# Graph layers: the receivers' offsets made in two parts, first head first

## The reference, cut to what matters

```python
def gat_conv(x, src, dst, W, att_src, att_dst, bias):
    N = x.shape[0]
    h = (x @ W).reshape(N, HEADS, HID)            # HEADS 4, HID 256, N 1250
    a_src = jnp.sum(h * att_src, axis=-1)
    a_dst = jnp.sum(h * att_dst, axis=-1)
    e = jax.nn.leaky_relu(a_src[src] + a_dst[dst], NEG_SLOPE)      # 0.2
    m = jax.ops.segment_max(e, dst, num_segments=N)
    e = jnp.exp(e - m[dst])
    s = jax.ops.segment_sum(e, dst, num_segments=N)
    alpha = e / (s[dst] + 1e-16)
    msg = alpha[:, :, None] * h[src]
    out = jax.ops.segment_sum(msg, dst, num_segments=N)
    return out.reshape(N, HEADS * HID) + bias
```

## Time and profile before

| what | value |
|---|---|
| median of 3 runs | 2343.44 us (2342.75 to 2345.57) |
| the profiled execution | 2332.56 us |
| its span | 2330.8 us |
| TensorE matmuls busy | 1995.9 us, 86% of the span |
| VectorE busy | 1480.5 us, 64% |
| ScalarE busy | 1132.7 us, 49% |
| layer 1, from its first rows to its last step | about 1336 to 1636 us |
| layer 2 | about 1636 to 1989 us |

### The profile page before, as it was taken

The page is one execution under the profiler, slowest core; times in us unless marked ns, Lnnn a source line. Parts: engine busy times, 40 slices in busy tenths (PEclk is TensorE's granted clock), DMA queues, the critical chain, the costliest instruction groups (busy, mean ns, idle before and its releaser), DMA issues. The chain is left out here.

```text
span 2330.8 us, 36639 instructions
## 1 busy us (share of the span) xinstructions
PE 1995.9 (86%) x11260; PEld 1284.6 (55%) x11261; DVE 1480.5 (64%) x2465; ACT 1132.7 (49%) x2288; POOL 794.3 (34%) x630
## 2 busy tenths in 40 slices
PE   5899999999996829999975597999999999980997
PEld 2444444444444727777732444777344777540997
DVE  1299999999995874333348675777373777438011
ACT  5777777777773314555510514665002666210332
POOL 4188888888880012444453000000000000001453
PEclk9999999999998957999988698999999999995998
DMA  5565565555552424778544313000012100331894
GB/s 162 168 164 154 153 155 156 155 155 154 155 155 80 93 82 147 264 254 261 186 127 125 103 44 116 22 22 1 18 44 89 57 22 1 109 110 35 227 275 93
DMA packets 200742, 285.13 MB, mean 122 GB/s; under 512 B 116698, under 2 KB 128677, under 8 KB 196543
## 3 DMA queue, kind: packets, MB, share of 16 engines
q0 software_dynamic: 98272, 142.08, 22.0%
q1 hardware_dynamic: 100158, 137.67, 19.4%
q10 hardware_dynamic: 2209, 4.07, 0.5%
HBM read 233.52 MB, written 49.84 MB: 122 GB/s over the span
## 5 line engine op out<-in xcount | busy, mean ns | idle before, releaser
L565 POOL DMA_INDIRECT p_s<-node_table,e_src_rows x320 | 497.9, 1556 | 106.9 <-issue 106.9
L2007 PE MATMUL g_psO<-g_h,g_ring 125*125 125x257 f32 x1600 | 372.7, 388 | 20.0 <-DVE g_ring L2139 10.6
L2007 PEld LDWEIGHTS g_psO<-g_h,g_ring 125*125 125x125 f32 x1600 | 296.8, 190 | 92.4 <-DVE g_stage L2133 26.6
L703 PE MATMUL p_psW<-e_w,p_hid 64*125 64x512 f32 x640 | 274.6, 652 | 39.6 <-ACT z L580 25.3
L622 DVE TENSOR_TENSOR g_b<-z,p_s 125x1536 f32<-125x1536 f32 x160 | 273.1, 1746 | 0.0
L711 PE MATMUL p_psM<-g_b 125*32 125x384 f32 x648 | 244.9, 525 | 15.3 <-DVE g_b L622 6.5
L580 ACT ACTIVATE z<-p_psW 125x512 f32<-125x512 f32 x320 | 186.7, 583 | 132.3 <-PE p_psW L703 132.3
L715 PE MATMUL p_psM<-g_b 125*32 125x256 f32 x648 | 216.3, 418 | 0.0
L714 PE MATMUL p_psM<-g_b 125*32 125x256 f32 x648 | 207.6, 404 | 0.0
L713 PE MATMUL p_psM<-g_b 125*32 125x256 f32 x648 | 190.8, 421 | 0.0
L585 ACT ACTIVATE p_of<-e_node_ids,z 125x314 bf16<-125x314 f16 x320 | 176.0, 550 | 9.2 <-PE p_psC L720 5.9
(11 more groups left out here) (357 smaller groups left out, 3756.8 us busy)
## 6 DMA issues: line engine op xcount, KB each, us to landing
p_ring<-in_L_ffn_weights SPq DMA_DIRECT2D x32, 1025.0 KB, 7.2
slot_rows<-p_y POOLq DMA_DIRECT2D x70, 256.0 KB, 4.4
p_w1s<-in_L_ffn_w SPq DMA_DIRECT2D x16, 1024.0 KB, 8.9
g_a<-in_L_ffn_w SPq DMA_DIRECT2D x16, 1024.0 KB, 7.0
hidden<-g_b SPq DMA_DIRECT2D x40, 250.0 KB, 3.3
p_hid<-hidden SPq DMA_DIRECT2D x160, 62.5 KB
g_rb<-receiver_rows SPq DMA_DIRECT2D x16, 610.4 KB
p_s<-node_table,e_src_rows POOLq DMA_INDIRECT x320, 5.1
```

The source lines that it names most:

```text
L565: pool.indirect_dma_start(s[:, g % 4, c, :, :].rearrange("p k u -> p (k u)"), None, node_table, bass.IndirectOffsetOnAxis(ap=src_rows[:, g ...
L703: nc.tensor.matmul(psW[c % 2][0:P, :], hid[part, b, c // 2, :], w4[part, :], start=True, stop=True)\
L2007: last = nc.tensor.matmul(psO[0:P, j, 0:HW], ring[:, i % RING, j * P:(j + 1) * P], h[:, s, hd, :], start=s == 0, stop=s == T - 1)
```

## The change

It splits the receivers' offsets into those of head 0 and those of heads 1 to 3. VectorE makes head 0's behind the ten maxima of head 0, and the other heads' behind all 40. TensorE turns the first part behind tile 4 (`MID` is 5 in place of `LATE`, 8) and the second behind the last tile; ScalarE copies the second part behind the first two `below`. SyncE writes and reads head 0's offsets between the loads of the senders' rows of heads 2 and 3. The senders' rows move to `rb[:, 1, 0]` and `rb[:, 1, 1]`, so head 1's load now waits until `ar`, which lies in the latter, has been turned. The order of `rr` and of the rows in memory becomes head, kind, tile, so that a row of 1250 lies in one piece there.

```diff
-        EARLY, LATE = 3 if vectors else 0, 8
+        EARLY, MID = 3 if vectors else 0, 5
-        rr = sb("rr", [P, T, 2, HEADS])
+        rr = sb("rr", [P, HEADS, 2, T])
-        rrt = sb("rrt", [T * 2 * HEADS, P])
+        rrt = sb("rrt", [(HEADS - 1) * 2 * T, 2, P])
...
+                rows = receiver_rows.rearrange("(r t) p -> r t p", t=T)
+                def receivers_in(hd):
+                    for k in range(2):
+                        sp.dma_start(rb[:, hd % 2, k, :].rearrange("p (t n) -> p t n", t=T),
+                                     rows[2 * hd + k].partition_broadcast(P)).then_inc(rb_in[hd % 2], 16)
                 for hd in range(HEADS):
+                    if hd == 1:
+                        sp.wait_ge(asd_mm, 1)
                     if hd >= 2:
                         sp.wait_ge(max_ok, (hd - 1) * T)
-                    sp.dma_start(rb[:, hd % 2, 0, :], sender_rows[hd].partition_broadcast(P)).then_inc(rb_in[hd % 2], 16)
-                sp.wait_ge(rrt_ok, 1)
-                sp.dma_start(receiver_rows, rrt[:]).then_inc(rr_out, 16)
-                sp.wait_ge(rr_out, 16)
+                    sp.dma_start(rb[:, 1, hd % 2, :], sender_rows[hd].partition_broadcast(P))\
+                      .then_inc(senders_in[hd % 2], 16)
+                    if hd == 2:
+                        sp.wait_ge(rrt_ok, 1)
+                        sp.dma_start(receiver_rows[0:2 * T, :], rrt[0:2 * T, 0, :]).then_inc(rr_out, 16)
+                        sp.wait_ge(rr_out, 16)
+                        receivers_in(0)
+                sp.wait_ge(rrt_ok, 2)
+                sp.dma_start(receiver_rows[2 * T:2 * T * HEADS, :], rrt[:, 1, :]).then_inc(rr_out, 16)
+                sp.wait_ge(rr_out, 32)
                 sp.wait_ge(max_ok, HEADS * T)
-                rows = receiver_rows.rearrange("(t r) p -> r t p", t=T)
-                for hd in range(HEADS):
+                for hd in range(1, HEADS):
                     if hd >= 2:
                         sp.wait_ge(bent, (hd - 1) * 2 * T)
-                    for k in range(2):
-                        ...
+                    receivers_in(hd)
...
-                head_rows(EARLY + 1, LATE)
+                head_rows(EARLY + 1, MID)
                 pe.wait_ge(rr_ok, 1)
                 pe.wait_ge(asd_ok, 1)
-                nc.tensor.transpose(psX[0:T * 2 * HEADS, 0, 0:P], rr[:]...)
+                nc.tensor.transpose(psX[0:2 * T, 0, 0:P], rr[:, 0, :, :]...)
                   .then_inc(rr_mm, 1)
-                head_rows(LATE, T)
+                head_rows(MID, T)
+                pe.wait_ge(rr_ok, 2)
+                nc.tensor.transpose(psX[0:(HEADS - 1) * 2 * T, 1, 0:P], rr[:, 1:HEADS, :, :]...).then_inc(rr_mm, 1)
...
                 below(0)
                 below(1)
+                act.wait_ge(rr_mm, 2)
+                nc.scalar.activation(rrt[:, 1, :], psX[0:(HEADS - 1) * 2 * T, 1, 0:P], ACT.Copy).then_inc(rrt_ok, 1)
...
+                def receivers(a, b):
+                    v.wait_ge(max_ok, b * T)
+                    top, high = peak[:, :, a:b], asd[:, :, 1, a:b]
+                    n = tick(nc.vector.tensor_tensor(top, most[:, :, a:b], high, ALU.add))
+                    tick.wait(n)
+                    n = tick(nc.vector.scalar_tensor_tensor(top, top, 0.2, top, ALU.mult, ALU.max))
+                    tick.wait(n)
+                    nc.vector.scalar_tensor_tensor(rr[:, a:b, 0, :]..., top, 1.0, high, ALU.add, ALU.subtract)
+                    nc.vector.scalar_tensor_tensor(rr[:, a:b, 1, :]..., top, 1.0, low[:, :, a:b],
+                                                   ALU.add, ALU.subtract).then_inc(rr_ok, 1)
...
+                    if hd == 0:
+                        v.wait_ge(asd_ok, 1)
+                        tick(nc.vector.tensor_scalar(as_low[:], asd[:, :, 0, :], 0.2, None, ALU.mult))
+                        tick(nc.vector.tensor_scalar(as_neg[:], asd[:, :, 0, :], -1.0, None, ALU.mult))
+                        tick(nc.vector.tensor_scalar(low[:], asd[:, :, 1, :], 0.2, None, ALU.mult))
+                        receivers(0, 1)
+                receivers(1, HEADS)
```

More of the change, by code:

```diff
@@ L1889, in graph_attention @@
         asd_ok = sem("asd_ok")
+        senders_in = [sem(f"senders_in{b}") for b in range(2)]
         rb_in = [sem(f"rb_in{b}") for b in range(2)]
@@ L1976, in _ @@
                 last.then_inc(asd_mm, 1)
[L1977 removed]
+                head_rows(EARLY + 1, MID)
                 pe.wait_ge(rr_ok, 1)
                 pe.wait_ge(asd_ok, 1)
[L1980 removed]
+                nc.tensor.transpose(psX[0:2 * T, 0, 0:P], rr[:, 0, :, :].rearrange("p k t -> p (k t)"), ident[0:P, 0:P])\
                   .then_inc(rr_mm, 1)
[L1982 removed]
+                head_rows(MID, T)
+                pe.wait_ge(rr_ok, 2)
+                nc.tensor.transpose(psX[0:(HEADS - 1) * 2 * T, 1, 0:P],
+                                    rr[:, 1:HEADS, :, :].rearrange("p h k t -> p (h k t)"), ident[0:P, 0:P])\
+                  .then_inc(rr_mm, 1)
                 def turn(u):
@@ L1987, in turn @@
                     if u == 0:
-                        pe.wait_ge(rrt_ok, 1)
+                        pe.wait_ge(rrt_ok, 2)
                     else:
@@ L2049, in _ @@
                    .then_inc(asd_ok, 1)
-                head_rows(EARLY + 1, LATE)
+                head_rows(EARLY + 1, MID)
                 act.wait_ge(rr_mm, 1)
-                nc.scalar.activation(rrt[:], psX[0:T * 2 * HEADS, 0, 0:P], ACT.Copy).then_inc(rrt_ok, 1)
-                head_rows(LATE, T)
+                nc.scalar.activation(rrt[0:2 * T, 0, :], psX[0:2 * T, 0, 0:P], ACT.Copy).then_inc(rrt_ok, 1)
+                head_rows(MID, T)
                 def below(i):
@@ L2086, in _ @@
                         attention_vectors(nc, v, wa_ok, ws, att, prod, wa, k)
+                def receivers(a, b):
[5 more added lines that the diff above has]
+                    tick.wait(n)
+                    nc.vector.scalar_tensor_tensor(rr[:, a:b, 0, :].rearrange("p h t -> p t h"), top, 1.0, high,
+                                                   ALU.add, ALU.subtract)
+                    nc.vector.scalar_tensor_tensor(rr[:, a:b, 1, :].rearrange("p h t -> p t h"), top, 1.0, low[:, :, a:b],
+                                                   ALU.add, ALU.subtract).then_inc(rr_ok, 1)
                 for hd in range(HEADS):
-                    v.wait_ge(rb_in[hd % 2], 16 * (hd // 2) + 16)
+                    v.wait_ge(senders_in[hd % 2], 16 * (hd // 2) + 16)
                     for t in range(T):
@@ L2097, in _ @@
                             out=ring[:, 2 * (i % 2):2 * (i % 2) + 2, :].rearrange("p a n -> p (a n)"),
-                            in0=rb[:, hd % 2, 0, :], in1=far[:, t, :], scale=1.0, scalar=FAR, op0=ALU.subtract, op1=ALU.max,
+                            in0=rb[:, 1, hd % 2, :], in1=far[:, t, :], scale=1.0, scalar=FAR, op0=ALU.subtract, op1=ALU.max,
                             accum_out=most[:, t, hd:hd + 1]).then_inc(max_ok, 1)
[L2100 to L2110, removed]
-                nc.vector.scalar_tensor_tensor(rr[:, :, 1, :], peak[:], 1.0, low[:], ALU.add, ALU.subtract).then_inc(rr_ok, 1)
+                    if hd == 0:
[5 more added lines that the diff above has]
+                receivers(1, HEADS)
                 def bend(i):
```

6 lines of the change are left out of this document (2 added, 4 removed).

## The result

The changed kernel takes 2328.32 us (median of 5 runs, 2325.27 to 2328.88) against 2342.75 us of the kernel before (median of 5, 2338.84 to 2345.57). The ratio is 0.9938, with a 95% interval of 0.9924 to 0.9951, so 14.4 us less, with 11.5 to 17.8 in the interval. The forecast was 10.1 us less, 2333.3, with a range down to 2329.5. The direction held, and the time lies 1.2 us under the range. (The forecast started from a median of 2343.44; measured beside the changed kernel it was 2342.75, so 0.7 us of the 5.0 between forecast and time are the starting point.)

What follows compares the result with a forecast made beforehand. TensorE was taken as the bound, with about 11 us in layer 1 waiting or slow. Layer 1's gain of 10.1 us, layer 2 at 0, took the median from 2343.44 to 2333.3 us, range 2329.5 to 2338.0.

Steps and rivals of the forecast that it cites:

- Layer 2: Attention's start in layer 2: offsets already early, only ScalarE's second copy on the path; 0 us taken, 0.3 as bound.
- Head 1's receivers: Layer 1 loads of head 1's receivers' rows: landed at 1435.3, with slack of over 30 us.
- the pieces: Layer 1 receivers' loads: still ten pieces of 500 bytes at 96 GB/s, 6.5 us each, giving a gain of 10.1 us.
- the rival with 0.25: Joined pieces, receivers' loads: rows in one piece run at the senders' rate; 10.9 us gained, 2332.5 us; chance 0.25.
- the path of VectorE: Layer 1: VectorE idles 6.9 us for head 3's senders, ends at 1418.1 and sets the first `bend`; gain 10.1 us.
- the path of ScalarE: Layer 1: both `below` through at 1417.8, then second copy and table load; exponential at 1419.4, a gain of 10.9 us.
- the slow restart: Layer 1, TensorE's two tiles after the wait: the lower clock costs 1.7 us, which the change saves.
- the clock term: TensorE's idle before attention's first matmul: where the clock falls and rises may shift; 1.7 us on either side.
- the same distance: Whole kernel: the median of runs lies 10.9 us above the profiled execution, taken alike for the changed kernel.
- Later senders: Rival, layer 1 loads: fixed parts don't overlap, head 3's senders land 4 us later; gain 6.1, 2337.3 us; chance 0.13.
- Nothing gained: Rival: something the split doesn't move holds attention, gain lost in a stall at step 20 or earlier; 2343.4 us; chance 0.03.
- slower: Rival, layer 1: head 3's senders at half rate behind two loads, first `bend` 7.8 us later; 2351.2 us; chance 0.03.

Runs made afterwards that it cites:

- e3: Changed kernel with offset rows in memory ordered head, tile, kind, so a row lies in ten pieces; ratio 0.9941 against the kernel before.
- e6: Kernel before with only the row order changed, so each row lies in one piece; ratio 0.9995 against the kernel before.
- e12: Kernel before, no edit, timed against itself beside the changed kernel on one chip; ratio 1.0001.
- e1: Kernel before, no edit, timed against itself and profiled again; ratio 0.9999.
- e9: Changed kernel, no edit, timed again on another chip; 2331.07 us against 2343.64 for the kernel before, ratio 0.9943.
- e4: Changed kernel with the first turning one tile later, behind tile 5 (MID 6); 2327.47 us, ratio 0.9971 against the kernel before.
- e7: Kernel before with joined rows and all offsets turned behind the last tile, unsplit; 2351.35 us, ratio 1.0084 against the kernel before.

## Why the prediction was right or wrong

**Right: where.** All of the gain that a profile can place is in layer 1, in TensorE's wait and slow restart. What failed is sizes in the sum, and with them the lower end of the range: the sum had 10.1 us where the profiles show 11.6 to 12.3 in the stretch, and the medians 13.3 in the mean and 14.4 in the first comparison. The tiles were forecast to end 70.6 us after the first one started, and ended at 70.4. Layer 2 gained and lost nothing: its added copy of 0.26 us took the place of idle time, of which 0.17 is left. Head 1's receivers and the next layer's weights were never waited for.

**Wrong, a size: the pieces.** "I take the slower rate, which is measured on the same tile with the same ten pieces in the instruction." The changed kernel moves joined rows at the senders' rate, the rival with 0.25. The instruction names ten pieces on either side; what counted was whether they lie one behind the other in memory. By e3 this is worth 0.7 us at the first `bend` and 0.8 at attention's first matmul; the forecast had 0.8. (Two loads of 625,000 bytes at 96 GB/s are 13.0 us and not 12.9, which changes nothing.) I leaned on the Trainium skill there, page "DMA: Bandwidth & Descriptors", section "Why a DMA increments its semaphore by 16 and not by 1", that one descriptor moves one contiguous run of the last dimension. The measurement decides against my use of it: an access written with a last dimension of 500 bytes was issued as quickly as a row of 5000 and moved at its rate.

**Wrong, a size: the path of VectorE.** In e3, which has the slow pieces, the first `bend` came at 73.05 us where my working gives 1418.1 - 1344.4 = 73.7. Head 3's first maximum came 0.55 us sooner than I had it, 58.5 us after the first tile in place of 59.0. The mechanism was right in each step (idle ahead of head 3, VectorE and not ScalarE last, TensorE waiting at the second turning).

**Wrong, a size: the path of ScalarE.** With the quick loads my working gives 10.9 us at the first exponential; it was 1430.28 - 1344.39 = 85.9 us after the first tile before, and is 1425.06 - 1350.65 = 74.4, so 11.5. Of the 0.6 us, 0.2 are the tiles, 0.25 the time from the last tile to the first `below`, for which I took the 1.26 us of the first profile and which is 1.0 in the others, and 0.1 the two `below`.

**Wrong, a size: the slow restart.** I priced it from one row, 15.54 - 13.8 = 1.7 us, and used this as the bound of the clock term too. Three more profiles with the wait (e6, e12, e1) give 15.65, 16.58 and 16.64 us, so 1.8 to 2.8. Since the change takes the restart away, the gain in the stretch is 11.6 to 12.3 us, not a constant; I had looked for this spread on the other side, in attention's start. There nothing moved one way: attention of layer 1 takes 196.6 to 197.7 us in the three profiles of the kernel before and 196.4 to 197.8 in the four of the changed one.

**Wrong: the range.** The forecast stood on one execution of the kernel before and on "the same distance" to the median. Executions and chips differ by as much, and where it can be seen the difference lies ahead of layer 1: on one chip the kernel before had a median of 2334, on another of 2344, and on the latter the changed kernel's first tile started at 1354.48 (e9), against 1347.10 and 1339.14 elsewhere, with the same time from there to the end within 2 us. The distance itself did no harm, but the range covered only the terms of my sum and a spread of 2.8 us seen in three runs. Four comparisons of the same two kernels spread over 3.4 us, and the first lay in the upper part of that. With 12 us in the stretch and that spread below it, the range should have gone down to about 2343.4 - 12 - 3.4 = 2328. That is said in hindsight, and up to 2.4 us of the mean gain have no cause that a run shows.

**The rivals.** "Later senders" did not come: three loads took 17.0 us, end to end, with their fixed parts paid once. "Nothing gained" and "slower" did not come; but e4 shows the mechanism of the latter with its point: 2.2 us of slack, and beyond it 4.5 of 6.9 us are paid. e7 shows another way to a slower kernel, the whole round trip behind the tiles, in both layers; it is no rival of this change, which splits the trip.

## What to carry to other kernels

If a chain of small results, a write to memory and a load back stands between two stages, split it so that what the next stage needs first goes round early, beside the work of the stage before; closing the engine's gap alone, without the split, made this kernel slower by 0.8%. A load put ahead of others in a queue has a price only beyond the slack of who waits for them: read that slack as the time between the last producer's end and the start of the consumer. And this gap on TensorE, of 9.2 to 9.5 us, cost its length and a restart of another 1.7 to 2.8 us, so take several profiles before pricing one.

## What the runs showed of the hardware

A transfer written as ten pieces of 500 bytes for each partition ran at 112 to 135 GB/s and was issued in about 0.3 us when the pieces lay one behind the other on both sides (the changed kernel, e6), and at 96 to 106 GB/s, with 4.5 to 6.4 us for each issue behind the first, when they did not (e3, the kernel before).

Loads of one queue didn't simply go one behind the other. In e7 the next layer's weights were issued behind four loads of receivers' rows; from 1416 to 1420 the transfers ran at a share of 0.31 to 0.35, and from 1422 at 1.05, before head 0's pair had landed. That pair took 15.3 us from its issue where 12.4 were counted from loads behind which nothing large stood. That the weights' transfer slowed the pair fits these rows, and so does a share of it for head 1's two loads, which were issued right behind; no run took either away alone.

After the same wait of 9.2 to 9.5 us TensorE's granted clock stood at 0.5 (1.2 GHz), and it went back to 1.0 at 3.3 us into the next tiles in one execution and at 5.5 us in another. That alone makes the two tiles take 15.5 or 16.6 us in place of 13.8.
